# Linear-attention output ahead of the first block of a fused projection stage, its three steps on three pairs at once

## The reference, cut to what matters

```
# linear attention, per head: q_feat, kv and k_sum are known by now
denom = maximum(q_feat . k_sum, 1e-6)
out   = (q_feat @ kv) / denom
s     = out @ W_out                       # 256 x 256
# mixture of experts: each token has two expert rows and two gate values
ffn   = x1 + gate0 * exp_out[row0] + gate1 * exp_out[row1]
x     = x + s * silu(ffn)                 # the residual of layer 1
xn    = layernorm(x)
q, k, v = xn @ Wq, xn @ Wk, xn @ Wv       # 256 x 512 each
g     = silu(xn @ (quantised kernel + a @ b) + bias)
```

## Time and profile before

| | us |
|---|---|
| median of the three runs | 3108.98 |
| the three runs | 3108.89, 3108.98, 3117.94 |
| the profiled execution's own time | 3104.42 |
| its span, first to last instruction | 3102.5 |
| the first instruction of this stage on TensorE | 1682.74 |
| first projection of block 0 (`qA 0`) | 1750.87 |
| last projection of the stage begins | 1965.25 |

### The profile page before, as it was taken

One profiled execution on the slowest core, in us unless ns is written; L12 is line 12 of the kernel. 1 busy time (PEld: TensorE's weight loads), 2 busy tenths in 40 slices (PEclk: granted clock), 3 DMA queues, 4 the chain that ended last, 5 costly groups with the idle time before them and its releaser, 6 DMA issues. The chain is left out here.

```text
span 3102.5 us, 46462 instructions
## 1 busy us (share of the span) xinstructions
PE 2850.2 (92%) x18025; PEld 1325.8 (43%) x18025; DVE 2022.6 (65%) x4462; ACT 1520.9 (49%) x2473; POOL 929.4 (30%) x420
## 2 busy tenths in 40 slices
PE   7897999999999963999998799799999999999987
PEld 4664233333333341676666555333333333333326
DVE  6886899999999555000001655588887877878823
ACT  3432577677677741222221444245565665565560
POOL 0001000000000022110001320166777777777780
PEclk9998799999999986999999999899999999999998
DMA  3223222022220034222112344421120220211005
GB/s 123 79 61 90 45 42 46 12 45 49 46 46 12 12 112 117 68 72 85 61 48 80 96 149 144 114 62 39 31 62 12 66 62 8 63 35 42 8 10 174
DMA packets 143625, 196.08 MB, mean 63 GB/s; under 512 B 14000, under 2 KB 109056, under 8 KB 141472
## 3 DMA queue, kind: packets, MB, share of 16 engines
q1 hardware_dynamic: 130304, 170.77, 19.8%
q0 software_dynamic: 6144, 16.79, 2.2%
q10 hardware_dynamic: 6960, 5.58, 0.6%
HBM read 116.81 MB, written 75.76 MB: 62 GB/s over the span
## 5 line engine op out<-in xcount | busy, mean ns | idle before, releaser
L912 ACT ACTIVATE at_probs<-at_st 128x512 f32<-128x512 f32 (+3 forms) x1280 | 588.3, 541 | 444.6 <-PE at_st L998 284.1
L874 POOL TENSOR_TENSOR at_probs<-at_probs 128x2048 f32<-128x2048 f32 (+3 forms) x208 | 732.9, 3528 | 220.6 <-ACT at_probs L912 136.8
L383 DVE TENSOR_REDUCE at_part<-at_s 128x1 f32<-128x512 f32 (+3 forms) x1280 | 689.2, 602 | 67.9 <-PE at_s L421 29.8
L365 ACT ACTIVATE at_probs<-at_st 128x1024 f32<-128x1024 f32 (+3 forms) x640 | 541.6, 895 | 275.9 <-PE at_st L440 138.1
L938 DVE TENSOR_REDUCE at_part<-at_s 128x1 f32<-128x512 f32 x768 | 498.4, 683 | 68.6 <-PE at_s L990 64.6
L990 PE MATMUL at_s<-at_kT,at_qT 96*128 96x512 f16 (+3 forms) x1280 | 391.4, 361 | 28.5 <-DMA at_kT<-klo 10.1
L998 PE MATMUL at_st<-at_qT,at_kT 98*128 98x512 f16 (+3 forms) x1280 | 379.3, 356 | 15.1 <-ACT at_probs L912 10.5
L421 PE MATMUL at_s<-at_kT,at_qT 48*128 48x512 f16 (+3 forms) x1280 | 359.6, 366 | 26.4 <-DMA at_qT<-qhi 10.2
L932 DVE CUSTOM_DVE_ANT_0 at_s<-at_s,at_later 128x384 f32<-128x384 f32 (+3 forms) x512 | 246.8, 497 | 109.4 <-PE at_s L990 109.0
L507 PE MATMUL at_acc<-at_probs,at_v 128*32 128x512 f32 (+3 forms) x2560 | 304.5, 549 | 8.9 <-ACT at_otile L352 8.8
L2319 DVE TENSOR_TENSOR ex_ot<-ex_bank,lin_b 128x512 f32<-128x512 f32 x32 | 22.1, 692 | 437.8 <-PE ex_bank L2349 437.8
(11 more groups left out here) (322 smaller groups left out, 3229.9 us busy)
## 6 DMA issues: line engine op xcount, KB each, us to landing
att<-at_otile SPq DMA_DIRECT2D x64, 256.0 KB, 2.1
lin_w<-in_W SPq DMA_DIRECT2D x16, 1024.0 KB, 7.7
at_v<-v SPq DMA_DIRECT2D x14, 1024.0 KB, 14.4
v<-pr_vt SPq DMA_DIRECT2D x32, 256.0 KB, 3.2
exp_out<-ex_ot SPq DMA_DIRECT2D x32, 256.0 KB, 2.1
v<-p_vt SPq DMA_DIRECT2D x32, 256.0 KB, 3.7
fi_a<-att SPq DMA_DIRECT2D x8, 1024.0 KB, 6.0
at_qT<-qhi SPq DMA_DIRECT2D x14, 512.0 KB, 9.3
```

The costliest lines, as they stand in the source:

```text
L365: act.activation(probs[:, quad % RING, heads_down * p:heads_down * (p + 1), off:QB], st_ps[n % st_slots][:, :, off:QB], ACT.Exp, scale=EXP ...
L383: dve.tensor_reduce(part[:, w % 2, qt * HG + h, j:j + 1], s_ps[n % S_SLOTS][:, 0:width], AX.X, ALU.max).then_inc(item_free, 1)
L874: pool.tensor_tensor(total, total, probs[:, slots.slot[quad], :, off:QB], ALU.add).then_inc(add_done, 1)
L912: act.activation(probs[:, slots.slot[quad], h, off:QB], st_ps[n % ST_SLOTS][:, off:QB], ACT.Exp, scale=EXP_SCALE).then_inc(exp_done, 1)
```

## The change

All 16 pairs stand ahead of block 0. On TensorE, round m is now `num m`, `nT m-1`, `s m-2`, and `T 0` comes ahead of `s 15`. ScalarE copies in the order `nT m+1`, `s m`, with silu 0 behind `s 7`, the square root of block 0 behind `s 10` and silu 1 behind `s 13`. VectorE mixes one tile of block 0 behind each of `nrm 4` to `nrm 7`, two tiles of block 1 behind `nrm 8` and `nrm 9`, block 0's combination behind `nrm 10`, its statistics behind `nrm 11`, the last two tiles of block 1 behind `nrm 12`, z of block 0 behind `nrm 13`, and the combination and statistics of block 1 behind `nrm 15`. No instruction is added or taken away on an engine. The parts of the diff that only rewrite the lists of names for ScalarE and VectorE in the same orders are left out.

```diff
--- before.py
+++ after.py
@@ -2375,33 +2375,22 @@
                         w_saved, w_kept):
     WID = P + 8
     PAIRS = NT // 2
-    FIRST = 11
-    after_turn, after_v = {0: (11, 12), 1: (13,), 2: (14,), 3: (15,)}, {}
-    lin_order = list(range(FIRST)) + [m for b in sorted(after_turn) for m in after_turn[b]]
-    assert lin_order == list(range(PAIRS))
     s_all = mix[:, :, :, :].rearrange("p t c n -> p t (c n)")
 
     pe_names, act_names, dve_names, jobs = [], [], [], []
-    numerators, values = [], []
-
-    def lin_pe(m):
-        pe_names.append(f"num {m}")
-        jobs.append((f"num {m}", "dve", f"nrm {m}"))
-
-    def lin_rest(m):
-        pe_names.extend([f"nT {m}", f"s {m}"])
-        jobs.append((f"s {m}", "act", f"s {m}"))
-
-    for m in range(FIRST):
-        lin_pe(m)
-        if m:
-            lin_rest(m - 1)
-    lin_rest(FIRST - 1)
-    pe_names += ["T 0"]
+
+    for m in range(PAIRS + 2):
+        if m < PAIRS:
+            pe_names.append(f"num {m}")
+            jobs.append((f"num {m}", "dve", f"nrm {m}"))
+        if 0 < m <= PAIRS:
+            pe_names.append(f"nT {m - 1}")
+        if m == PAIRS + 1:
+            pe_names.append("T 0")
+        if m > 1:
+            pe_names.append(f"s {m - 2}")
+            jobs.append((f"s {m - 2}", "act", f"s {m - 2}"))
     for b in range(NB):
-        for m in after_turn.get(b, ()):
-            lin_pe(m)
...
@@ -2468,11 +2455,7 @@
         part_out, v_kept, ch, least_ready = (c.sem(n) for n in ("part_out", "v_kept", "ch", "least_ready"))
         pe_s, act_s, dve_s = Marks(c.sem("pe"), pe_names), Marks(c.sem("act"), act_names), Marks(c.sem("dve"), dve_names)
         marks = {"act": act_s, "dve": dve_s}
-        turns = [(f"nT {m}", (act_s, f"nT {m}")) for m in range(FIRST)] + [("T 0", (act_s, "T 0"))]
-        for b in range(NB):
-            turns += [(f"nT {m}", (act_s, f"nT {m}")) for m in lin_of(b)]
-            if b + 1 < NB:
-                turns += [(f"T {b + 1}", (act_s, f"T {b + 1}"))]
+        turns = [(f"nT {m}", (act_s, f"nT {m}")) for m in range(PAIRS)] + [(f"T {b}", (act_s, f"T {b}")) for b in range(NB)]
         rot = Banked(c, "rot", turns, 1)
         banks = Banked(c, "bank", [(n, (marks[e], d)) for n, e, d in jobs], 3)
         block = c.block()
@@ -2523,12 +2506,14 @@
         def _(act):
             step = act_s.step
 
-            def lin(m):
+            def linear(m):
                 pe_s.wait(act, f"nT {m}")
                 if m >= 2:
                     pe_s.wait(act, f"s {m - 2}")
                 step(f"nT {m}", act.activation(nT[:, m % 2, :, :, :].rearrange("p t c n -> p (t c n)"),
                                                rot.tile(f"nT {m}")[:, 0, :], ACT.Copy))
+
+            def output(m):
                 pe_s.wait(act, f"s {m}")
                 step(f"s {m}", act.activation(s_all[:, 2 * m:2 * m + 2, :].rearrange("p t n -> p (t n)"),
                                               banks.tile(f"s {m}")[:, 0, :], ACT.Copy))
@@ -2554,20 +2539,21 @@
                 step(f"hi {job}", act.activation(parts[:, side, 0, f:f + 2, :], banks.tile(job)[:, :, :], ACT.Copy,
                                                  scale=scale_qk[side]))
 
-            for m in range(6):
-                lin(m)
-            silu(0)
-            for m in range(6, 9):
-                lin(m)
-            deviation(0)
-            silu(1)
-            for m in range(9, FIRST):
-                lin(m)
-            turned(0)
+            linear(0)
+            for m in range(PAIRS):
+                if m + 1 < PAIRS:
+                    linear(m + 1)
+                else:
+                    turned(0)
+                output(m)
+                if m == 7:
+                    silu(0)
+                if m == 10:
+                    deviation(0)
+                if m == 13:
+                    silu(1)
             deviation(1)
             for b in range(NB):
-                for m in lin_of(b):
-                    lin(m)
                 if b + 2 < NB:
                     silu(b + 2)
                 if b:
@@ -2607,17 +2593,23 @@
                               d[:, y].unsqueeze(3).to_broadcast([P, NF, 8, 16]), ALU.mult)
                 step(f"nrm {m}", last)
 
+            def mixed_tile(b, t):
+                n = 4 * b + t
+                if b >= 2 and t == 0:
+                    dve_s.wait(dve, f"x {b - 2}")
+                dve.wait_ge(got[n % 8], 32 * (b // 2 + 1))
+                link(stt(out=fg[:, b % 2, t, :], in0=rows[:, b % 2, t, 0, :], scalar=gate[:, 0, n:n + 1],
+                         in1=x_all[:, n, :], op0=ALU.mult, op1=ALU.add))
+                last = stt(out=fg[:, b % 2, t, :], in0=rows[:, b % 2, t, 1, :], scalar=gate[:, 1, n:n + 1],
+                           in1=fg[:, b % 2, t, :], op0=ALU.mult, op1=ALU.add)
+                if t < 3:
+                    link(last)
+                else:
+                    step(f"mixed {b}", last)
+
             def mixed(b):
-                if b >= 2:
-                    dve_s.wait(dve, f"x {b - 2}")
                 for t in range(4):
-                    n = 4 * b + t
-                    dve.wait_ge(got[n % 8], 32 * (b // 2 + 1))
-                    link(stt(out=fg[:, b % 2, t, :], in0=rows[:, b % 2, t, 0, :], scalar=gate[:, 0, n:n + 1],
-                             in1=x_all[:, n, :], op0=ALU.mult, op1=ALU.add))
-                    last = stt(out=fg[:, b % 2, t, :], in0=rows[:, b % 2, t, 1, :], scalar=gate[:, 1, n:n + 1],
-                               in1=fg[:, b % 2, t, :], op0=ALU.mult, op1=ALU.add)
-                step(f"mixed {b}", last)
+                    mixed_tile(b, t)
 
             def combine(b):
                 cols = slice(4 * b, 4 * b + 4)
@@ -2626,6 +2618,9 @@
                 link(tt(fg[:, b % 2, :, :], fg[:, b % 2, :, :], s_all[:, cols, :], ALU.mult))
                 dve.wait_ge(x_ld[b % 2], 16 * (b // 2 + 1))
                 step(f"x {b}", tt(x_all[:, cols, :], fg[:, b % 2, :, :], xs[b % 2][:, :, :], ALU.add))
+
+            def statistics(b):
+                cols = slice(4 * b, 4 * b + 4)
                 dve_s.wait(dve, f"x {b}")
                 for t in range(4 * b, 4 * b + 4):
                     last = dve.bn_stats(stats[:, t, :], x_all[:, t, :])
@@ -2654,20 +2649,24 @@
 
             dve.memset(least[:, :], FLOOR).then_inc(least_ready, 1)
             dve.wait_ge(least_ready, 1)
-            for m in range(6):
+            for m in range(PAIRS):
                 normalise(m)
-            mixed(0)
-            for m in range(6, 9):
-                normalise(m)
-            combine(0)
-            mixed(1)
-            for m in range(9, FIRST):
-                normalise(m)
-            normalised(0)
+                if 4 <= m < 8:
+                    mixed_tile(0, m - 4)
+                if m in (8, 9):
+                    mixed_tile(1, m - 8)
+                if m == 10:
+                    combine(0)
+                if m == 11:
+                    statistics(0)
+                if m == 12:
+                    mixed_tile(1, 2)
+                    mixed_tile(1, 3)
+                if m == 13:
+                    normalised(0)
             combine(1)
+            statistics(1)
             for b in range(NB):
-                for m in lin_of(b):
-                    normalise(m)
                 if b + 1 < NB:
                     normalised(b + 1)
                 if b + 2 < NB:
@@ -2677,6 +2676,7 @@
                 lower(1, "k", "A", b)
                 if b + 2 < NB:
                     combine(b + 2)
+                    statistics(b + 2)
                 lower(1, "k", "B", b)
                 pe_s.wait(dve, f"y {b}")
                 if b:
@@ -2725,19 +2725,16 @@
                         mm = pe.transpose(d[:, f, t * P:(t + 1) * P], z[:, t, f * P:(f + 1) * P], C["identf"][:, :])
                 step(f"T {b}", mm)
 
-            for m in range(FIRST):
-                numerator(m)
-                if m:
+            for m in range(PAIRS + 2):
+                if m < PAIRS:
+                    numerator(m)
+                if 0 < m <= PAIRS:
                     linear(m - 1)
-                    project(m - 1)
-            linear(FIRST - 1)
-            project(FIRST - 1)
-            turn(0)
+                if m == PAIRS + 1:
+                    turn(0)
+                if m > 1:
+                    project(m - 2)
             for b in range(NB):
-                for m in lin_of(b):
-                    numerator(m)
-                    linear(m)
-                    project(m)
                 act_s.wait(pe, f"T {b}")
                 if b == 0:
                     pe.wait_ge(w_ld[0], 48)
```

More of the change, by code:

```diff
@@ L2377, in combine_and_project @@
     PAIRS = NT // 2
-    FIRST = 11
-    after_turn, after_v = {0: (11, 12), 1: (13,), 2: (14,), 3: (15,)}, {}
-    lin_order = list(range(FIRST)) + [m for b in sorted(after_turn) for m in after_turn[b]]
-    assert lin_order == list(range(PAIRS))
```

(36 more changed lines are left out.)

## The result

| | before | changed |
|---|---|---|
| median of four runs each, us | 3112.51 | 3087.17 |
| lowest and highest | 3108.89, 3117.94 | 3082.70, 3095.93 |
| ratio changed to before | | 0.9923, 95% interval 0.9909 to 0.9937 |
| stage: first `num` to the start of the last `y`, from the profiled executions | 1965.25 - 1682.74 = 282.5 | 1953.77 - 1694.18 = 259.6 |

The change makes the kernel faster: 0.77%, between 0.63 and 0.91. The medians lie 25.3 us apart, with 26 forecast, and the measured time lies 4 us above the predicted one, inside the range; 3.5 of the 4 us are the kernel before, whose median is 3112.51 with a fourth run and was 3108.98 with three. The profiled execution of the changed kernel is the slowest of its four, 3095.93 us, only 8.5 under that of before.

A forecast was written before the change was run, and what follows sets the result against it. TensorE, busy 92%, was taken as the bound, idle at waits for ScalarE's copy and VectorE's division. Gains of 10.3 (front, after kB 0's stall) and 16.0 (blocks 1 to 3) summed to 26.3 us: 3083 us, range 3075 to 3093.

The forecast's parts named there:

- a round: TensorE's pairs: num 0.92, four transposes 0.44 and product 1.80 sum to 3.16 us a round, against 4.10 before.
- pairs, gained up to `qA 0`: TensorE's front: `qA 0` starts at 1739.0 instead of 1750.87, 11.9 us gained.
- wait of kB 0: Block 0 on TensorE: kB 0 stalls 1.6 us for its PSUM tile, until the lower half of qA 0 is out.
- blocks 1 to 3, gained: Blocks 1 to 3 lose their late pairs, 18.0 us, and give back 1.95 for mixing no longer hidden: net 16.0.
- cross-check from the waits: Whole stage: idleness, low clock and transposes' tails removed, less new waits of 6.4, give a gain of 23.4 us.
- costs of nothing: Gathers, loads, stores and table loads: same number and order or early enough, so no cost.
- rival C: Low clock: stalls of 0.9, 1.5 and 1.6 us each bring a slow stretch, 5 us more, 3088; chance 0.11.
- what is late next: Chain from silu 1's end to qA 0's lower half: 15.2 us, out at 18.3, so kB 0 stalls 1.6.
- Rival B: Rounds 10 to 15: VectorE's extras delay the divisions and set the pace; gain 17, 3092 us; chance 0.17.
- Rival D: VectorE waits for gathered rows before the first mixed tile; no change, 3109 us at 26 lost; chance 0.05.
- rival E: Denser rounds run at the 1.2 GHz level, 6.3 us each; slower, 3133 us if all 16; chance 0.03.
- rival F: ScalarE: a table switch holds it 1.28 us longer than its row; gain 23.4, 3086 us; chance 0.03.

The follow-up runs named there:

- Experiment 3: Changed kernel with all pairs ahead but the rounds in series again (num m, nT m-1, s m-1); stage 278.1 us against the changed kernel's 259.6.
- experiment 4: Changed kernel with overlapped rounds for 13 pairs only, pairs 13, 14 and 15 back at the heads of blocks 1 to 3; stage 273.4 us.
- Experiment 1: Changed kernel without the extra chain step behind the first three tiles of each mixed block; stage 255.5 us against 259.6.
- Experiment 2: Changed kernel with silu 1 one place earlier on ScalarE, behind s 12 instead of s 13; stage 256.6 us against 259.6.
- 8: Changed kernel again, unaltered, on a second chip; ratio to the kernel before 0.9920, stage 280.0 us.
- Experiment 12: Changed kernel with silu 1 behind s 12 and block 1's square root ahead of the copy of s 15; wait of kB 0 0.49 us.
- experiment 11: Changed kernel with the loads of Wq, Wk and Wv waiting for num 7, on a third chip; stage 277.6 us, long stall 9.2 us.

## Why the prediction was right, and where its terms were off

Its steps, each against the trace of the changed kernel:

| term, us | forecast | measured |
|---|---|---|
| a round | 3.16 | 3.09 |
| waits for the division, rounds 12 to 15 | 0.9 and 0.4 | 0.88 and 0.27 |
| wait of `T 0` | 1.5 | 1.47 |
| pairs, gained up to `qA 0` | 11.9 | 68.1 - 55.5 = 12.6 |
| wait of kB 0 | 1.6 | 1.86 |
| block 0, lost | 1.6 | 3.8 |
| blocks 1 to 3, gained | 16.0 | 3 x 30.92 - 3 x 25.96 = 14.9 |
| blocks 4 and 5, lost | 0 | 2 x 0.37 = 0.75 |
| stage | 26.3 | 22.9 |

The mechanism held. TensorE no longer waits for the copy, the division is late only behind the combination and the statistics and behind z 0, and the late pairs' 5.99 us went. Experiment 3 shows that the overlap is most of it, and experiment 4 that the last rounds cost less than their length.

How close the times came is in part luck. The sum was 26.3 and the stage, which it was a sum of, gained 22.9; the medians gained 25.3, and nothing in the change explains the 2.4 us between. The cross-check from the waits (23.4) lies nearer, but it had left out the second slow stretch of the kernel before (1747.48, 1.6 us), which went too and makes it 25.0.

Three terms were mis-sized. The product in a round was taken from a round with a wait, 1.80; without one it is 1710.62 - 1708.89 = 1.73, 0.07 a round, about the 0.7 us that the pairs gained beyond the forecast. The part "costs of nothing" missed that the new `mixed_tile` links the second product of tiles 0 to 2, where the old loop linked none: 0.12 us three times a block, and no slack behind it in blocks 0 to 5, 6 x 0.37 = 2.2 us together. Experiment 1 shows it. And block 0 met rival C once: a stretch at a granted clock of 0.64 over kB 0, which is partly the 1.2 GHz level, for 1.7 us (5.40 instead of 3.70). I had given it three such stretches at 0.11; one came. The stretch of the kernel before at 1747.48, behind waits of 1.46 and 0.78 us, spoke for this rival and was overlooked. What decides was not found out: the length of the wait alone does not, for kB 0 waited 1.86 us in experiment 4 as well, and 1.5 to 1.8 in experiments 1, 2 and 8, without it:

```profile
1757.14 3.70 PE L2771 MATMUL p_bank<-p_xT,p_w 128*128 128x512 f32 x8 [1.86 <-DVE p_parts L2663]
```

The 3.8 us of block 0 are this 1.7 and the wait, which costs 1.86 + 0.27 = 2.1; the forecast of 1.6 was 0.5 short, 0.37 of it the links.

One step was right by chance. The chain to kB 0 was put on silu 1, in the part "what is late next". Experiment 2 moved silu 1 by three us and left kB 0's wait at 1.78: the square root behind the copy of `s 15` holds it as long. The prediction had it at 0.3 together with the hand-overs, without its place behind the copy and its table load. In the changed kernel both chains happened to end at the same time, so the size of the term was right and its cure was not. Experiment 12 confirmed it.

Rival B (VectorE sets rounds 10 to 15) did not happen; waits of 1.1 us in all speak against it, and experiment 4 shows where it would: with fewer rounds. Rival D's waits for the gathered rows do not appear in the trace of the changed kernel. The low clock of rival E came in none of the rounds behind the first (granted 0.99 from 1697.4 to 1743.7). The longer switch of rival F does not show: silu 0 runs at 1725.10 behind a table load of 1.28 us that began at 1723.81.

## What to carry to other kernels

When three engines pass a tile on, start the next tile's first step before the last tile's final one: it turned 4.10 us a round into 3.09, most of it idle time of the bound engine. Before taking work out of a front for its length, ask what it covers: three rounds of 3.09 us cost 1.1 to 4.1 together here, not 9.3, since another engine's work had to end there anyway. And read a rewritten helper for its waits, not only its instructions: three waits of 0.12 us in a loop without slack cost 0.37 a block. In a chain of handovers a tiny step (a square root of 0.2 us with its table load of 1.28) placed behind a copy that comes late holds all that follows. And when two chains end at the same time, moving one shows only that the other is there.

## What the runs showed of the hardware

- The same kernel was 21 to 24 us slower on two other chips (before: 3112 against 3136 and 3133). In seven traces of the changed kernel and its versions there, and in that of the kernel before, TensorE, ScalarE and VectorE stand some 10 us, between 8 and 25 us into this stage, released by nothing that the profile shows; the first traces and experiments 1 to 4 have none of it. It does not hang on the 1.5 MB of weights loaded at that time (experiment 11). What it is stays open; whether the gathers have a part in it was not tried.
- The ratio to the kernel before stayed 0.992 on the first and the second chip, although the stage gained 22.9 us on the one and 297.5 - 280.0 = 17.5 by single traces of the third and the second. Single traces differ by several us, outside the stage and on those chips inside the pairs too, so this is no contradiction that the runs could resolve.
- A wait of one and the same length brought a slow stretch or none: 1.86 us at kB 0, then 5.40 us for eight records in the changed kernel and 3.70 in experiment 4.
- A link (an instruction's own increment, waited for by the next on the same engine) cost 0.12 us on VectorE: tiles 1.03 apart with it, 0.91 without.
